# A third buffer for the q and k rows in a fused attention and expert layer: row transfers spread over the slots, expert weights issued by ScalarE

## The chip, the cores and the metric

The kernel runs on one core of one Trainium2 chip. The metric is the device time of one execution in microseconds (us). A profile records one execution; its span runs from the first to the last instruction. PE is TensorE, PEld its weight load, DVE VectorE, ACT ScalarE, POOL GpSimd, SP SyncE; SPq and ACTq are the sequencers of SP and ACT, where DMA issues stand.

## What is computed

The input is 1024 tokens of width 256, layer-normed, and the output adds two branches to it. Cut to what matters:

```python
q, k, v = heads(xn @ Wq.T), heads(xn @ Wk.T), heads(xn @ Wv.T)      # 16 heads of 16
scores = einsum('bhid,bhjd->bhij', q, k) / sqrt(16)                  # 1024 x 1024, causal
std_out = out_proj(softmax(masked(scores)))
qg, qd = splat_feats(q); kg, kd = splat_feats(k)                     # 8 "splats" a head: exp and tanh
splat_attn = (amps*qg) @ kg.T + strength * (amps*qg*qd) @ (kg*kd).T
gsa_out = out_proj(softmax(masked(scores + sensitivity * splat_attn)))
attn = (1 - blend) * std_out + blend * gsa_out
# experts: 16, top 2 of sqrt(softplus(xn @ gate_w.T)), at most 128 tokens each
h = silu(buf @ W1.T) * (buf @ W3.T);  out = h @ W2.T                 # 256 -> 176 -> 256
shared = (silu(xn @ Ws1.T) * (xn @ Ws3.T)) @ Ws2.T
return x + attn + gathered(out) + shared
```

## The kernel before

**Prologue.** The tokens are normed, transposed and projected to q and k (`proj`), the splat features of q and of k are made from these (`feat`), then v and the gate's logits. Attention needs q, k and features as bf16, so each float32 half (q, k, q features, k features, two halves each: eight in all, the order is `SPLIT_ORDER`) is split into three bf16 parts whose sum is the float: ACT writes part 0 (`part0`), a subtraction makes the rest (`rest_of`), ACT writes part 1 (`part1`), and another subtraction makes part 2 (`third_of`, signalled by `part_done`). DVE does six of the first subtractions and two thirds; POOL does six thirds (`POOL_THIRDS` and `LATE`) and the first subtraction of the two late halves (`late_rest_of`). `product(s)` multiplies two features on DVE.

**Rows.** A matmul of a head contracts over 96 rows in SBUF: the three parts of 16 dimensions, repeated so that the wanted products of parts meet, and two rows more for a shift. DMAs copy the parts from `split` into the tiles of the list `stage`: `qs` and `ks` (q and k rows), `fq` and `fk` (feature rows). `RUNS` says which parts go to which rows. One group of two heads takes 12 DMAs of q and k (`load_rows`, `load_qk`), 18 of features (`load_features`) and one for two rows of `fq` (`load_gaps`). Each tile holds two groups: `pr = g % 2` is the group in use, `1 - pr` the next. SP issues all q and k rows and the features of a group's first head; POOL issues the features of the second head.

**Maxima and shift.** Softmax is made safe by the row maxima of the scores, which are found one group ahead. The tasks `max2` and `max` are matmuls on PE into a PSUM bank and a DVE reduction of it; they need the next group's q and k rows (`qk_in`). `shift` turns the maxima (`mhl`, `mT`), and `shift_rows` writes them as two rows under `qs`.

**Main loop.** There are 8 groups. A group has 6 pairs of key blocks, a pair has 4 slots, so 24 slots. In each pair PE runs `pv` of the pair before (weights times v), `splat(0)`, `splat(1)` (adds the feature product to the scores in PSUM), then `std(0)` and `std(1)` of the next pair (q times k). ACT takes the exponential of the scores after `std` and again after `splat`. `splat` waits for the first exponential, the next `std` for the second, `pv` for both. Other work is put into slots by hand in `PLAN`: at slot n of a group every engine does its part of the tasks listed there. The lists are these: maxima of the next group in slots 5 to 7 and 9 to 19, shifts in 9 and 21; routing in group 0; the shared expert in groups 0 and 1 (`sgu`, `shT`, `sy`); four experts in each of the groups 2 to 5 with `xT`, `gu`, `hT`, `y` at slots f+1, f+2, f+4, f+5 for f = 0, 5, 10, 15; the additions of expert outputs in the groups 6 and 7. A `gu` is a matmul on PE, a tanh on ACT, two multiplications on DVE. Three PSUM banks serve these tasks in turn (`place`).

**SP's order.** SP reads the same plan. In group g it first waits until all splats of group g-1 are done (`gsa_ready`) and issues its share of the features of g+1. At `shift` it waits for the shift and issues two small DMAs; at `y` it waits for the expert's output, stores it, and issues the weights of expert a+3 (`expert_in`, two DMAs into the buffer that expert a has just left). At slot 21 (`RELOAD`) it waits until all `std` of the group are done and issues the 12 rows of q and k of group g+2, into the buffer that group g has just left:

```python
if at == RELOAD and g + 2 < NG:
    sp.wait_ge(std_ready, (g + 1) * NU)
    load_qk(g + 2, g % 2)
```

Since group g+1 starts right after slot 23 of group g, and its slot 5 needs these rows, they have some five slots.

**A branch.** If a bound on the features is large (`wide`), a slow way to find the maxima is taken. With these inputs it is not; PE, DVE and SP each load the flag and jump over that code. On PE and DVE the jump stands right ahead of the main loop; the code jumped over is written out eight times, once a group.

## Time and profile before

| | us |
|---|---|
| median of 3 runs | 453.52 (452.94 to 457.52) |
| the profiled execution | 457.28 |
| its span | 455.5 |
| PE busy in it | 353.4 (78%) |
| DVE busy | 233.8 (51%) |
| ACT busy | 194.5 (43%) |
| POOL busy | 114.8 (25%) |
| granted TensorE clock, mean | 0.875 |

All times below are of the profiled execution, counted from the start of its span. A clock of 1.00 is 2.4 GHz, 0.50 is 1.2 GHz. The prologue takes until 83 us; the main loop starts with the first `std` at 83.31. Groups then begin at about 136, 182, 231, 279, 328, 378 and 416 us.

### The profile page before, as it was taken

The page shows a single profiled execution, that of the slowest core. Times are in us where ns is not written, and L with a number is a line of the kernel's source. Part 1 is how long each engine was busy: PE and PEld are TensorE (multiplying, and loading weights), DVE is VectorE, ACT ScalarE, POOL GpSimd, SP SyncE. Part 2 cuts the span into 40 slices and gives each one's busy share as a digit, 9 for nine tenths or more (in the row PEclk, how much of TensorE's full clock was granted, in tenths as well). Part 3 has the DMA queues.
Part 4 walks back from the last instruction along what each step waited for, and adds up shares of the span by engine and source line. Part 5 has one row for each costly group of instructions (what it writes and reads, how often), then busy time and mean ns, then how long its engine had stood idle before and what let it go on. Part 6 is the DMA issues. An engine that isn't in the chain of part 4 may idle for free.

```text
span 455.5 us, 6183 instructions
## 1 busy us (share of the span) xinstructions
PE 353.4 (78%) x2172; PEld 178.8 (39%) x2172; DVE 233.8 (51%) x609; ACT 194.5 (43%) x277; POOL 114.8 (25%) x158
## 2 busy tenths in 40 slices
PE   1996962598975989599976988499928995698984
PEld 1532730244433534254434444344515442333442
DVE  5436579157742664256533664275515751477413
ACT  1874733343433344425350455044522535266830
POOL 5211563400057341400050005010310008720000
PEclk9997955578989799969995999799986999599996
DMA  6233230640035351752275425543385006620011
GB/s 194 95 44 60 26 61 1 81 58 8 0 97 76 43 47 51 110 101 81 72 143 71 141 72 108 89 110 106 88 95 104 21 13 110 171 56 3 0 47 46
DMA packets 28131, 33.02 MB, mean 72 GB/s; under 512 B 8033, under 2 KB 21537, under 8 KB 28097
## 3 DMA queue, kind: packets, MB, share of 16 engines
q1 hardware_dynamic: 21601, 25.16, 25.5%
q0 software_dynamic: 5072, 7.38, 11.5%
q8 instruction: 19, 0.31, 0.3%
q10 hardware_dynamic: 1424, 0.04, 0.2%
q14 instruction: 15, 0.12, 0.1%
HBM read 15.60 MB, written 4.28 MB: 44 GB/s over the span
## 4 chain that ended last, share of the span: by engine, by line
PE 55%; SPq 15%; DVE 14%; ACT 6%; DMA 5%; issue 4%; DVEq 0%; ACTq 0%
SPq L293 13%; PE ps L821 11%; PE ps L749 6%; DVE mx L1096 5%; PE ps L792 5%; PE ps L722 5%; PE ps L758 5%; ACT arena_p L640 5%; PE ps L804 4%; DMA stage<-split 3%; PE ps L680 3%; PE ps L777 2%; PE ps L699 2%; DVE w_sb L917 1%; PE ps L762 1%
## 5 line engine op out<-in xcount | busy, mean ns | idle before, releaser
L640 ACT ACTIVATE arena_p<-ps 128x1024 f32<-128x1024 f32 (+1 forms) x192 | 147.4, 811 | 125.7 <-PE ps L804 97.4
L1096 DVE TENSOR_REDUCE mx<-ps 128x1 f32<-128x512 f32 (+3 forms) x160 | 89.4, 592 | 35.0 <-PE ps L724 29.2
L821 PE MATMUL ps<-arena_p,v_full 128*32 128x512 f32 (+3 forms) x768 | 74.7, 508 | 0.6 <-ACT arena_p L640 0.6
L722 PE MATMUL ps<-stage 96*128 96x512 bf16 (+3 forms) x160 | 57.8, 399 | 13.4 <-DVE mx L1096 11.2
L792 PE MATMUL ps<-stage 98*128 98x512 bf16 (+1 forms) x192 | 54.9, 354 | 15.5 <-ACT arena_p L640 10.9
L804 PE MATMUL ps<-stage 98*128 98x512 bf16 (+1 forms) x192 | 48.8, 340 | 4.5 <-ACT arena_p L640 4.1
L301 POOL DMA_DIRECT2D stage<-split x48 | 27.0, 620 | 76.9 <-PE ps L804 65.3
L387 POOL DMA_INDIRECT wt<-xn_scratch,ids_sb x16 | 15.7, 984 | 116.7 <-PE ps L739 111.5
L645 ACT ACTIVATE small<-ps 128x176 f32<-128x176 f32 x24 | 7.6, 318 | 79.1 <-PE ps L749 79.1
L714 PE MATMUL ps<-stage 96*128 96x128 bf16 (+1 forms) x32 | 8.4, 337 | 42.0 <-DMA stage<-split 42.0
L722 PEld LDWEIGHTS ps<-stage 96*128 96x128 bf16 x160 | 16.9, 109 | 46.0 <-issue 23.3
L821 PEld LDWEIGHTS ps<-arena_p,v_full 128*32 128x32 f32 x768 | 20.4, 111 | 36.2 <-issue 31.2
L758 PE MATMUL ps<-arena_o,small 88*128 88x256 f32 x96 | 30.3, 444 | 4.3 <-DVE small L1119 4.2
L792 PEld LDWEIGHTS ps<-stage 98*128 98x128 bf16 x192 | 19.6, 104 | 35.1 <-ACT arena_p L640 15.7
L1091 DVE TENSOR_REDUCE mx<-ps 128x1 f32<-128x128 f32 x16 | 4.6, 288 | 44.3 <-PE ps L716 44.3
L795 PE MATMUL ps<-mask_t,ident_b 128*128 128x128 bf16 x128 | 26.5, 226 | 0.0
L395 POOL DMA_INDIRECT ids_scratch<-tok,sidx x16 | 15.5, 967 | 43.2 <-DVE sidx L1050 38.6
L804 PEld LDWEIGHTS ps<-stage 98*128 98x128 bf16 x192 | 16.1, 102 | 24.9 <-issue 12.4
L724 PE MATMUL ps<-mask_n,ident_b 128*128 128x128 bf16 x96 | 24.1, 251 | 0.0
L758 PEld LDWEIGHTS ps<-arena_o,small 88*128 88x128 f32 x96 | 18.5, 213 | 13.0 <-DVE small L1119 8.7
L749 PE MATMUL ps<-w_sb,wt 128*128 128x352 f32 x64 | 22.9, 481 | 0.0
L348 POOL TENSOR_TENSOR split<-rest,split 128x1024 bf16<-128x1024 f32 x6 | 12.9, 2152 | 36.2 <-ACT split L582 29.3
(190 smaller groups left out, 466.2 us busy)
## 6 DMA issues: line engine op xcount, KB each, us to landing
w_sb<-in_w_dram SPq DMA_DIRECT2D x16, 352.0 KB
stage<-split SPq DMA_DIRECT2D x40, 96.0 KB
arena_o<-in_w_dram SPq DMA_DIRECT2D x16, 176.0 KB
stage<-split SPq DMA_DIRECT2D x40, 64.0 KB
ye_scratch<-wt SPq DMA_DIRECT2D x16, 128.0 KB, 1.8
stage<-split SPq DMA_DIRECT2D x56, 32.0 KB
acc<-in_x_dram SPq DMA_DIRECT2D x2, 512.0 KB, 4.5
wt<-in_wqkvo_dram SPq DMA_DIRECT2D x4, 256.0 KB, 6.4
```

Source lines behind the costliest of these rows:

```text
L293: eng.dma_start(stage[n][row:row + num * HD, pr, h, :], src).then_inc(done, 16)
L301: eng.dma_start(stage[n][row + w:row + num * HD:2, pr, h, :], split[p0:p0 + NS, 2, part:part + 1, w, :].to_broadcast((NS, num, T))).then_i ...
L640: A(to, ps[:, 1 + 2 * s:3 + 2 * s, off:CH], ACT.Exp, scale=SCALE).then_inc(done, 1)
L722: ins = M(b[:, 0:n1 - n0], lhs, ks[0:KR, pr, h, n0:n1], start=True, stop=not diag)
L724: ins = M(b[:, n1 - n0 - P:n1 - n0], ident_b[:, :], mask_n[:, :], start=False, stop=True)
L749: ins = M(b[:, 0:2 * I], lhs, w13_sb[:, wb, k, :], start=k == 0, stop=k == KD - 1)
L758: ins = M(b[:, 0:D], hT[:, c, :], w2_sb[:, wb, c, :], start=c == 0, stop=c == 1)
L792: ins = M(b[:, off:CH], ks[:, pr, h, (jb + s) * P:(jb + s + 1) * P], qs[:, pr, h, ic * CH + off:(ic + 1) * CH], start=True, stop=not diag)
L795: ins = M(b[:, off:off + P], ident_b[:, :], mask_t[:, :], start=False, stop=True)
L804: ins = M(ps[:, 1 + 2 * s + h, off:CH], fk[:, pr, h, (jb + s) * P:(jb + s + 1) * P], fq[:, pr, h, ic * CH + off:(ic + 1) * CH], start=Fals ...
L821: ins = M(ps[c:c + 2 * HD, 0, off:CH], v_full[:, jb + s, g * GH + h, :], of, start=jb + s == 0, stop=end)
L1096: V.reduce_max(mx[:, it // TC, h, it % TC, pc:pc + 1], b[:, 0:n1 - n0], AX.X).then_inc(aux_free, 1)
```

## The change

- `qs` and `ks` hold three groups (`QB = 3`), `g % QB` is the group in use. The 12 row transfers of group g+2 go out in slots 0 to 11 of group g, one a slot. The feature rows of both heads and the gap row (19 in all) go out in slots 2 to 20 of group g, one a slot, all from SP. The only wait ahead of them is `gsa_ready` at slot 0. POOL issues no rows.
- The weights of experts 3 to 15 are issued by ACT, in the slot of a `gu`, right behind its tanh. The weights of experts 0 to 2 stay with SP.
- The maxima lie in slots 0 to 5 and 6 to 20, the shifts in 8 and 22.
- Prologue: another `SPLIT_ORDER`, no `LATE` halves; DVE does all eight first subtractions and thirds 0 to 3, POOL thirds 4 to 7, and the rests of halves 4 to 7 lie in `arena_p`. PE makes both feature sets without a break, then takes the branch, then the first maxima (`max0`) and v. DVE takes the branch ahead of `max0`. In the branch PE and DVE run a hardware loop over the groups in place of the eight copies. SP issues the q and k rows of group 1 ahead of the features of group 0.

```diff
-        stage = [sb(f"stage{n}", [KS, 2, GH, T], bf16) for n in range(4)]
+        stage = [sb(f"stage{n}", [KS, QB if n < 2 else 2, GH, T], bf16) for n in range(4)]
...
-        SPLIT_ORDER = [(0, 0), (1, 0), (2, 0), (2, 1), (3, 0), (3, 1), (0, 1), (1, 1)]
-        LATE = (6, 7)
-        POOL_THIRDS = (1, 2, 3, 5)
+        SPLIT_ORDER = [(0, 0), (1, 0), (0, 1), (1, 1), (2, 0), (2, 1), (3, 0), (3, 1)]
+        POOL_THIRDS = (4, 5, 6, 7)
...
-        maxima = spread(max0, 5, 7) + [(9, ("shift", 0))] + spread(max1, 9, 19) + [(21, ("shift", 1))]
-        RELOAD = 21
+        maxima = spread(max0, 0, 5) + [(8, ("shift", 0))] + spread(max1, 6, 20) + [(22, ("shift", 1))]
...
             for g in range(NG):
-                if g < NG - 1:
-                    if g:
-                        sp.wait_ge(gsa_ready, g * NU)
-                    load_features(sp, g + 1, 1 - g % 2, 2, F_SP, f_in[1 - g % 2])
-                    load_features(sp, g + 1, 1 - g % 2, 3, F_SP, f_in[1 - g % 2])
-                    load_gaps(g + 1, 1 - g % 2)
...
                             sp.dma_start(ye_d[a * CAP:(a + 1) * CAP, :], ye[:, a % YB, :]).then_inc(ye_out[a % YB], 16)
-                            if a + WB < E:
-                                expert_in(a + WB)
...
-                    if at == RELOAD and g + 2 < NG:
-                        sp.wait_ge(std_ready, (g + 1) * NU)
...
-                        load_qk(g + 2, g % 2)
+                    if g and at == 0:
+                        sp.wait_ge(gsa_ready, g * NU)
+                    if g + 2 < NG and at < N_QK:
+                        load_qk_row(sp, g + 2, (g + 2) % QB, at, qk_in[(g + 2) % QB])
+                    if g + 1 < NG and 2 <= at < 2 + N_F:
+                        load_feature_row(sp, g + 1, (g + 1) % 2, at - 2, f_in[(g + 1) % 2])
...
                                 A(th, ps[:, bank, 0:I], ACT.Tanh, scale=0.5).then_inc(th_ready, 1)
+
+                            if kind == "gu" and 1 <= a and a - 1 + WB < E:
+                                e = a - 1 + WB
+                                act.wait_ge(aux_free, count_of("y", a - 1))
+                                act.dma_start(w13_sb[:, e % WB, :, :], w13[e, :, :].rearrange("(k p) i -> p k i", p=P)).then_inc(w_in[e % WB], 16)
+                                act.dma_start(w2_sb[:, e % WB, :, :], w2[e, :, :].rearrange("(k p) d -> p k d", p=I2)).then_inc(w_in[e % WB], 16)
...
-                for g in range(NG):
-                    pe.wait_ge(own_in, (g + 1) * (16 * 30))
+                with pe.Fori(0, NG) as g:
+                    pe.wait_ge(own_in, (g + 1) * (16 * (N_QK + N_F - 1)))
...
+            pe.wait_ge(qk_in[0], 16 * N_QK)
+            for t in max0:
+                aux(-1, t, 0)
+            prologue(n_v)
+            aux(-1, ("shift", 0), 0)
```

Three places show what moved. The first is SP's queue at the end of a group with experts (`stage0` and `stage1` are `qs` and `ks`, `stage2` and `stage3` are `fq` and `fk`, L457 is the shift, L513 an expert's output). Before:

```order
L513 DMA ye_scratch<-wt 128x256 [waits aux_free]
L497 DMA w13_sb<-in_w13_dram 128x2x352
L498 DMA arena_o<-in_w2_dram 88x2x256
L457 DMA stage0<-mT 2x4x128 [waits aux_free]
L457 DMA stage0<-mT 2x4x128
L293 DMA stage0<-split 48x1x1024 [waits part_done7,part_done6,std_ready]
L293 DMA stage0<-split 32x1x1024
L293 DMA stage0<-split 16x1024
```

After, at the same place:

```order
L308 DMA stage3<-split 16x1x1024
L483 DMA ye_scratch<-wt 128x256 [waits aux_free]
L311 DMA stage2<-gap_scratch 2x2048
L427 DMA stage0<-mT 2x4x128 [waits aux_free]
L427 DMA stage0<-mT 2x4x128
L295 DMA stage0<-split 48x1x1024 [waits gsa_ready]
L295 DMA stage0<-split 32x1x1024
L295 DMA stage0<-split 16x1024
L302 DMA stage2<-split 24x1x1024
```

The weights are gone from the queue, the 12 rows no longer wait for the last `std` of their own buffer, and the gap row of the next group stands behind the wait for the group's last expert. The rows that follow are those of the group after the next.

The second is ACT in a group with experts (arena_p takes the exponentials, `small` the tanh). Before:

```order
L640 ACTIVATE arena_p<-ps 128x2x384 [waits std_ready]
L640 ACTIVATE arena_p<-ps 128x1024 [waits gsa_ready]
L645 ACTIVATE small<-ps 128x176 [waits aux_full]
L640 ACTIVATE arena_p<-ps 128x2x384 [waits gsa_ready]
L640 ACTIVATE arena_p<-ps 128x2x256 [waits std_ready]
```

After:

```order
L608 ACTIVATE arena_p<-ps 128x2x384 [waits std_ready]
L608 ACTIVATE arena_p<-ps 128x1024 [waits gsa_ready]
L613 ACTIVATE small<-ps 128x176 [waits aux_full]
L618 DMA w_sb<-in_w_dram 128x2x352 [waits aux_free]
L619 DMA arena_o<-in_w_dram 88x2x256
L608 ACTIVATE arena_p<-ps 128x2x384 [waits gsa_ready]
L608 ACTIVATE arena_p<-ps 128x2x256 [waits std_ready]
```

Two DMA issues stand between the tanh and the next exponential.

The third is DVE in the prologue (L924 and L896 are first subtractions, L1153 and L1126 the product, L1091 and L1096 reductions of the maxima). Before:

```order
L1153 SCALAR_TENSOR_TENSOR arena_o<-arena_o,par 128x1024 [waits pro_act]
L924 SCALAR_TENSOR_TENSOR rest<-arena_o,par,split 128x1024 [waits part_done0,first_part]
L924 SCALAR_TENSOR_TENSOR rest<-arena_o,split 128x1024 [waits part_done1,first_part]
L1091 TENSOR_REDUCE mx<-ps 128x1 [waits aux_full]
L1092 TENSOR_REDUCE mx<-ps 128x1
```

After:

```order
L889 TENSOR_TENSOR split<-rest,split 128x1024 [waits second_part,second_rest] x2
L1126 SCALAR_TENSOR_TENSOR arena_o<-arena_o,par 128x1024 [waits pro_act]
L896 SCALAR_TENSOR_TENSOR arena_p<-arena_o,par,split 128x1024 [waits first_part]
L896 SCALAR_TENSOR_TENSOR arena_p<-arena_o,split 128x1024 [waits first_part]
L889 TENSOR_TENSOR arena_o<-arena_o 128x1024 [waits pro_act]
L896 SCALAR_TENSOR_TENSOR arena_p<-arena_o,split 128x1024 [waits first_part] x2
L1142 TENSOR_LOAD wide [waits wide_ready]
L1142 ISA x2
L1143 COMPARE_AND_BRANCH
```

All subtractions and the branch now come ahead of the first reduction; before, the reductions of `max0` stood after four of them and the branch after all maxima.

## Rows read from the trace of the kernel before

**Rows 1.** The chain that ended last, by engine and by line, from the page.

```profile
PE 55%; SPq 15%; DVE 14%; ACT 6%; DMA 5%; issue 4%; DVEq 0%; ACTq 0%
SPq L293 13%; PE ps L821 11%; PE ps L749 6%; DVE mx L1096 5%; PE ps L792 5%; PE ps L722 5%; PE ps L758 5%; ACT arena_p L640 5%; PE ps L804 4%; DMA stage<-split 3%; PE ps L680 3%; PE ps L777 2%; PE ps L699 2%; DVE w_sb L917 1%; PE ps L762 1%
```

**Rows 2.** Waits: engine, line, releaser; us in total, times, longest us.

```profile
PE ps L714 <- DMA stage<-split: 42.0, 7, 8.7
ACT arena_p L640 <- PE ps L804: 97.4, 37, 11.3
```

**Rows 3.** Timeline of PE: start, us, engine, line; idle before and its releaser.

```profile
37.58 0.23 PE L714 MATMUL ps<-stage 96*128 96x128 bf16 x1 [3.22 <-DMA stage<-split]
...
148.06 0.29 PE L714 MATMUL ps<-stage 96*128 96x128 bf16 x1 [4.34 <-DMA stage<-split]
...
342.94 0.29 PE L714 MATMUL ps<-stage 96*128 96x128 bf16 x1 [8.67 <-DMA stage<-split]
```

**Rows 4.** Windows: us, busy us (instructions) of PE, PEld, DVE, ACT, POOL; PEclk, DMA share, GB/s.

```profile
148.00:158.00 10.00, 9.82 (x54) 5.58 (x55) 6.55 (x18) 3.66 (x5) 3.06 (x3) 0.70 0.34 35
...
194.50:204.00 9.50, 9.41 (x48) 5.69 (x48) 5.55 (x16) 1.64 (x4) 0.99 (x1) 0.61 0.52 89
...
243.20:251.40 8.20, 8.19 (x36) 5.09 (x40) 4.87 (x13) 0.80 (x3) 0.99 (x1) 0.61 0.45 61
251.40:281.50 30.10, 28.04 (x198) 14.16 (x199) 18.14 (x46) 15.94 (x21) 6.44 (x11) 1.00 0.38 106
...
391.60:400.00 8.40, 8.36 (x54) 4.44 (x55) 6.37 (x18) 4.45 (x5) 6.27 (x8) 0.72 0.61 146
```

**Rows 5.** Timeline of SP's queue, at the start of group 0 and from group 3 to 4.

```profile
81.02 12.93 SPq L293 DMA_DIRECT2D stage<-split  x12
...
276.56 0.34 SPq L513 DMA_DIRECT2D ye_scratch<-wt  x1
276.94 0.44 SPq L497 DMA_DIRECT2D w_sb<-in_w_dram  x1
277.42 0.44 SPq L498 DMA_DIRECT2D arena_o<-in_w_dram  x1
...
279.23 10.65 SPq L293 DMA_DIRECT2D stage<-split  x12
```

**Rows 6.** Timeline around one tanh and one expert's end: ACT and PE.

```profile
261.40 0.32 ACT L645 ACTIVATE small<-ps 128x176 f32<-128x176 f32 x1 [4.02 <-PE ps L749]
261.61 3.77 ACT L640 ACTIVATE arena_p<-ps 128x1024 f32<-128x1024 f32 x4
...
262.69 0.61 PE L804 MATMUL ps<-stage 98*128 98x512 bf16 x2 [0.40 <-ACT arena_p L640]
...
278.99 0.59 PE L804 MATMUL ps<-stage 98*128 98x512 bf16 x2
```

**Rows 7.** Timeline of the prologue: POOL and DVE.

```profile
60.91 4.21 POOL L355 TENSOR_TENSOR rest<-xx,split 128x1024 f32<-128x1024 f32 x2
...
61.93 3.35 DVE L1004 SCALAR_TENSOR_TENSOR w_sb<-w_sb 128x128 f32<-128x128 f32 x1
...
70.36 4.07 DVE L917 TENSOR_TENSOR w_sb<-w_sb 128x128 f32<-128x128 f32 x2
```

**Rows 8.** Timeline of the prologue: ACT, PE and DVE, and the branch.

```profile
37.64 1.06 ACT L582 ACTIVATE split<-rest 128x1024 bf16<-128x1024 f32 x1
...
48.37 7.17 PE L699 MATMUL ps<-wt,xx 128*128 128x256 f32 x32
55.38 4.03 PE L673 MATMUL ps<-gw_sb,xx 128*128 128x16 f32 x32
...
65.34 3.13 DVE L1096 TENSOR_REDUCE mx<-ps 128x1 f32<-128x512 f32 x6
...
83.29 0.29 DVE L917 TENSOR_TENSOR g_last<-w_sb,gb_sb 128x128 f32<-128x128 f32 x1 [3.74 <-issue]
...
83.31 0.58 PE L792 MATMUL ps<-stage 98*128 98x512 bf16 x1 [4.33 <-issue]
```

252 lines of the change are left out of this document (111 added, 141 removed).

## The prediction

> **What bounds the kernel now.** I read the chain that ended last first. PE carries 55% of the span, which is no surprise with PE busy for 78% of it; but SP's queue carries 15%, 13% of it at L293, the issue of q and k rows, and the row transfers another 3% [rows 1]. An engine that computes nothing holds some 18% of the time. The waits say where: PE at L714, the first maxima task of the next group, waits for a transfer into the row tiles seven times, 42.0 us in total [rows 2]. In PE's timeline one of the seven is in the prologue, 3.22 us; the other six are one in each of the groups 1 to 6, from 4.34 to 8.67 us [rows 3]. They add up to 42.0 - 3.2 = 38.8 us. Group 0 has none, and group 7 has no maxima.
>
> The cause stands in SP's queue. From group 3 to 4, the last expert's output goes at 276.56, its weights at 276.94 and 277.42, two shift rows follow, and only at 279.23 do the 12 rows start, which take 10.65 us [rows 5]. Group 4 has itself begun by then: its first `splat` runs at 278.99 [rows 6]. The rows are needed some five slots later and can't come earlier, since they go into the buffer that group 3 has just left.
>
> The windows show a second cost behind the wait. In the 8 to 10 us after each of the six waits the granted clock is between 0.61 and 0.72 (four of the six are shown), while in the rest of a group it is 1.00 [rows 4]. PE is busy without a gap there, 8.19 of 8.20 us from 243.2, so the time is PE's own work at a lower clock. At full clock a window of length w and clock c would take w x c: the loss is 3.0 us (10 x 0.30), 3.7, 3.2 and, in the last, 2.4 us; the two not shown give 2.8 each. That is 17.9 us. Of TensorE's two levels, 1.2 GHz is what is granted for most of these windows, after an idle stretch of 4 to 9 us.
>
> So a group of some 48 us holds about 6.5 us of wait and 3 us of slow clock. The undisturbed stretch from 251.4 to 281.5 has PE busy for 28.04 of 30.10 us at clock 1.00 [rows 4]: once the wait is gone, PE itself is the bound there.
>
> **The change part by part.**
>
> *Third buffer and spread rows.* The rows of group g+2 go out in the first half of group g, into a buffer that group g-1 has left, and are needed in slot 0 of group g+1. Twelve rows take 10.65 us on SP, and 12.93 at their slowest [rows 5], against a group of nearly 40 us. All six waits end: -38.8 us. With them goes the slow stretch: -17.9 us.
>
> *What SP now has to carry.* A group has 12 q and k rows, 18 feature rows (9 before) and the gap row. I have no row for 31 in a run, so bounds: at 10.65/12 = 0.89 us each they take 27.5 us, at 12.93/12 = 1.08 us each 33.4 us; four shift rows and four expert outputs add about 4. That is 32 to 37 us in a group that I expect to last about 42, so SP keeps up, but with little room. One place is tight. The gap row stands behind the wait for the last expert (slot 20), and the next group's first `splat` needs it. Before, the expert's output was issued at 276.56 and that `splat` ran at 278.99, 2.4 us later. The gap row would be issued next, at about 276.94, and take roughly 0.4 us to issue; of its landing I only know that output stores and rows land in about 2 us. It comes at about 279.4: 0.4 us late, in four or five groups. I put +2 us on this (0 to 5).
>
> *Expert weights on ACT.* Thirteen experts, each with two issues. On SP they took 0.44 us each [rows 5], so 0.9 us a pair and 11.7 us for all, now between a tanh and the next exponential. Is ACT's idle time the cover? ACT waits for PE's L804 for 97.4 us [rows 2], but not there: before its tanh it sits 4.02 us idle for the matmul of `gu`, while exponentials queue behind the tanh. After the one at 261.40 come four exponentials without a gap, 3.77 us, and PE's `splat` at 262.69 already waits 0.40 us for them [rows 6]. So a pair ahead of them is mostly on the path. Only in slot 7 does a long `pv` (slots 2, 12 and 17 have none between) give cover. I take 0.85 of 11.7: +10 us. Ends: 0 (all hidden) and 13 x 2 = +26 us, if an issue on ACT takes 1 us, the slowest row of SP's. The short wait it adds for the last expert's output costs nothing: DVE has done that before PE could start this `gu`, as `gu` waits for the later `xT`.
>
> A rule of the Trainium skill speaks here. *DMA: Bandwidth & Descriptors*, section on issuing engines, says that issues from several engines run on the same 16 DMA engines, and that using more of them only saves the issuing sequencer's time. The trace agrees as far as it goes (the same transfers in the window from 251.4 with a DMA share of 0.38), so the move to ACT earns nothing by itself.
>
> *Features off POOL.* POOL's issues were not on the chain [rows 1], 0.
>
> *Maxima over 21 slots instead of 14.* The tasks are the same. In the stretch after the wait DVE was busy for 4.87 of 8.20 us [rows 4], which would be nearly all of it once PE runs at full clock (8.2 x 0.61 = 5.0 us). Spreading them takes that away. I count 0, within 3 us.
>
> *Prologue.* This I worked out as a chain, and the result is nearly nothing. Before, DVE had its first late maxima at 59.9 and the last at 77.8, then the branch cost PE 4.33 us up to the first `std` at 83.31 and DVE 3.74 us [rows 8]. In that stretch DVE twice ran into POOL: a 128x128 operation of 0.3 us took 3.35 us beside POOL's 4.21, and two took 4.07 us [rows 7]. Some 6.5 us of that go, because POOL's work is done earlier. After, the steps are: (1) from 27 us ACT has 11 conversions of 1.06 us [rows 8], 8 feature evacuations of about 0.65 and two projections of 1.0, and waits for a product for about 2.5: 48 us; the last subtraction ends at 49. (2) The branch on DVE, 3.7 us: 52.7. (3) The first maxima and shift: 3.9 us, 56.7. (4) The v and gate matmuls, 7.17 + 4.03 = 11.2 us [rows 8], which ran beside ACT's and DVE's work before and now stand between the first and the later maxima. A quarter of v is ahead of the shift, but PE has sat idle for most of the time from 40 to 53, so I add about 3 us for a slow clock: 70. (5) Sixteen maxima at 3.13/6 = 0.52, with gaps 0.58 us, 9.3 us, and the gate's DVE work, 4.5 us: 83.9. The first `std` comes at about 84, against 83.31: +1 us. If the shorter code makes the jump cheap it is 81 (-2.5), if PE's clock stays low for all of v and gate 89 (+6).
>
> The lock between DVE and POOL is also in the Trainium skill (*SBUF — State Buffer*, on the shared port pair: an exclusive lock for a whole instruction). By a plain sharing of bandwidth the 0.3 us operations would take 0.6; the row shows 3.35, so the whole of the excess goes with the overlap.
>
> *Sum,* against the profiled execution: 457.3 - 38.8 - 17.9 + 2 + 10 + 1 = 413.6 us. That execution is 3.8 us above the median of 453.52. In proportion, 413.6 x 453.5 / 457.3 = 410.2; less the same 43.7 us, 409.8. I say 411.
>
> **The rivals.**
>
> *The ACT issues are hidden.* For it: 97.4 us of ACT waiting for PE [rows 2]. Against it: the queue of exponentials behind each tanh. Time: 411 - 10 = 401 us.
>
> *The wait moves to the feature rows.* SP has 31 rows a group and everything behind one queue, and the share of the DMA engines reached 0.52 even behind the waits [rows 4]. For it: the slowest rate shown, 1.08 us a row, brings SP to 37 us of 42. Against it: half the rows then have a group to spare. If PE waits 3 us for features at each of six starts, and gets the slow clock back for 2 us each time: +30, 441 us.
>
> *The clock gives back little.* The stretch after a wait could be paced by DVE's reductions or ACT's queue rather than by PE. For it: DVE 4.87 us in what would be 5.0. Against it: PE has no gap there. If only a quarter of 17.9 comes back: 411 + 13 = 424 us. A page of the Trainium skill points this way: *TensorE: Matmul & The Clock Gate*, section on HAM oscillation, has an example in which each wait for a transfer is followed by 1.67 us at half speed, half of which is lost; six of those would be 5 us, an estimate from the page, and the time by it 424. The windows here measure more, 17.9 us, and I go by them.
>
> *Nothing moves.* The transfers, not their issue, were late, and stay late under the same load: 453 us. Against it: the share of the DMA engines is only 0.38 in the stretch from 251.4 [rows 4], and the rows will go out there.
>
> *Slower.* Place: ACT, behind the tanh. If an issue on ACT is held while the DMA engines work off the rows that SP now sends all through the group, the exponentials behind it are late, and PE gets the lower clock as well, as it did behind the wait of 4.34 us. Price: a pair must cost 13 x p > 56.7 - 3, so p above 4.1 us. At p = 5 us, 454 - 57 + 3 + 65 = 465 us. Nothing shows such an issue: SP's own slowest, at a full load, is 1.08 us.
>
> **How the numbers follow.** Forecast 0.60; ACT hidden 0.12; wait at the features 0.14; clock gives back little 0.08; nothing 0.03; slower 0.03. The predicted time is the forecast's, 411. The range takes in the hidden ACT (401), the clock rival (424), the upper ends of the ACT price and of the prologue taken one at a time, and leaves out the 441: 400 to 429. A measurement of this kernel tells about 1% from no change. Faster by over 1%: 0.60 + 0.12 + 0.14 + 0.08 = 0.94; within 1%: 0.03; slower: 0.03.
>
> **What would show it.** Right: no wait of PE at the first maxima task for a transfer; a window of clock 1.00 through all of the groups 2 to 5; groups 2 to 5 of 42 to 43 us; ACT issues of 0.4 to 0.5 us on its queue and a PE wait for ACT of under 1 us behind each `gu`; a first `std` between 81 and 89. The ACT price is wrong if groups 2 to 5 are not 3 to 4 us longer than group 6, which has no experts. The whole is wrong if `splat(0)` of a group waits for a transfer for over 2 us, or if the clock stays under 0.8 without any wait.

## The result and the profile after

The changed kernel takes 411.88 us (median of 4 runs, 407.55 to 413.09) against 455.52 us before (median of 4). The ratio is 0.902, 95% interval 0.893 to 0.912. The profiled execution took 413.09 us, 44.2 us less than that of before (457.28). In the experiments one execution of `rows_burst` (566.19 us at a granted clock of 0.561) and two of `act_early_again` (397 us at 0.93) are left out of the ratios as slow. The forecast was 411, in a range from 400 to 429. The sum came out right; its terms did not, and two of them missed by 6 and 8 us in opposite directions.

The page of the profile after, engines and the chain that ended last (before: [rows 1]):

```profile
PE 339.2 (82%) x2172; PEld 173.6 (42%) x2172; DVE 234.2 (57%) x613; ACT 194.3 (47%) x277; POOL 66.2 (16%) x82
...
PE 67%; DVE 15%; ACT 10%; issue 3%; ACTq 3%; DMA 1%; DVEq 0%; SPq 0%
```

SP's queue went from 15% of the chain to nothing, PE from 55% to 67%. New is ACT's queue with 3%: some 12 us in which the end waited for a DMA issue on ACT.

The waits of PE after (us in total, times, longest; before: [rows 2]):

```profile
PE ps L766 <- ACT arena_p L608: 13.5, 15, 2.1
PE ps L778 <- ACT arena_p L608: 11.6, 12, 1.7
```

There is no row with a transfer any more; the 42.0 us at the first maxima are gone. At the top stand the matmuls of `std` (L766) and of `splat` (L778), waiting for exponentials.

The windows show where the time went. A stage ends where DVE copies the second shift (`mT`) of a group: the prologue, then groups 0 to 6; group 7 is the rest of the span. The bounds of these windows lie up to 0.7 us behind the copies. Columns as in [rows 4]. After:

```profile
0.00:78.30 78.30, 53.15 (x207) 29.00 (x208) 46.88 (x113) 40.39 (x59) 18.80 (x33) 0.84 0.41 80
78.30:127.70 49.40, 41.58 (x241) 20.06 (x242) 31.44 (x105) 20.78 (x30) 6.72 (x7) 0.84 0.30 55
127.70:168.60 40.90, 37.10 (x253) 18.90 (x251) 22.88 (x59) 19.12 (x28) 11.92 (x13) 0.96 0.35 60
168.60:214.80 46.20, 40.21 (x263) 20.23 (x262) 24.18 (x64) 19.55 (x28) 3.78 (x4) 0.93 0.41 90
214.80:257.80 43.00, 36.46 (x260) 18.87 (x258) 24.15 (x63) 19.55 (x28) 3.78 (x4) 1.00 0.46 113
257.80:302.10 44.30, 37.24 (x268) 19.76 (x266) 25.45 (x65) 19.66 (x28) 3.78 (x4) 1.00 0.47 109
302.10:343.20 41.10, 36.47 (x259) 18.87 (x258) 24.16 (x63) 19.34 (x28) 1.89 (x2) 1.00 0.40 85
343.20:370.70 27.50, 25.39 (x214) 11.56 (x212) 20.47 (x51) 18.06 (x25) 15.50 (x16) 1.00 0.45 112
```

From copy to copy groups 2 to 5 take 45.7, 43.0, 44.3 and 41.1 us, 174.1 in all. The same stages before took 79.3, 54.8, 46.2, 47.9, 48.2, 48.8, 50.6 and 38.6 us at clocks between 0.79 and 0.93. Group 7 did not change (41.1 and 40.9 us). So groups 1 to 6 gave back 280.3 - 243.0 = 37.3 us, and the prologue with group 0 gave 134.13 - 127.46 = 6.7 us. At full clock PE is busy for about 36.5 us in a group with experts, but groups 2 to 5 take 41 to 46 us. Group 1, with only the shared expert, takes 41.0. What lies between is the subject of the experiments.

### The profile page after: what moved, and what is told of

Read it like the earlier page. It is cut to its first block, busy times and chain, and to the rows that moved or that the text cites. A ratio compares the mean times of both kernels' runs of the same rounds, so it can differ in the third digit from the quotient of the medians.

```text
span 411.3 us, 6179 instructions
## 1 busy us (share of the span) xinstructions
PE 339.2 (82%) x2172; PEld 173.6 (42%) x2172; DVE 234.2 (57%) x613; ACT 194.3 (47%) x277; POOL 66.2 (16%) x82
## 4 chain that ended last, share of the span: by engine, by line
PE 67%; DVE 15%; ACT 10%; issue 3%; ACTq 3%; DMA 1%; DVEq 0%; SPq 0%
PE ps L795 16%; PE ps L723 8%; PE ps L766 7%; ACT arena_p L608 7%; DVE mx L1069 6%; PE ps L732 5%; PE ps L778 5%; PE ps L696 5%; PE ps L654 4%; ACTq L619 2%; PE ps L751 2%; PE ps L673 2%; PE ps L769 2%; ACT small L613 2%; PE ps L736 1%
## 5 line engine op out<-in xcount | busy, mean ns | idle before, releaser
L608 ACT ACTIVATE arena_p<-ps 128x1024 f32<-128x1024 f32 (+1 forms) x192 | 145.8, 811 | 96.6 <-PE ps L778 58.5
L1069 DVE TENSOR_REDUCE mx<-ps 128x1 f32<-128x512 f32 (+3 forms) x160 | 92.1, 592 | 78.2 <-PE ps L698 53.9
L766 PE MATMUL ps<-stage 98*128 98x512 bf16 (+1 forms) x192 | 51.9, 337 | 14.2 <-ACT arena_p L608 13.5
L778 PE MATMUL ps<-stage 98*128 98x512 bf16 (+1 forms) x192 | 46.8, 334 | 11.6 <-ACT arena_p L608 11.6
L370 POOL DMA_INDIRECT wt<-xn_scratch,ids_sb x16 | 15.2, 950 | 157.7 <-PE ps L713 154.5
L696 PEld LDWEIGHTS ps<-stage 96*128 96x128 bf16 x160 | 15.6, 99 | 45.7 <-issue 26.2
L766 PEld LDWEIGHTS ps<-stage 98*128 98x128 bf16 x192 | 18.6, 100 | 34.1 <-ACT arena_p L608 22.4
L732 PE MATMUL ps<-arena_o,small 88*128 88x256 f32 x96 | 27.8, 415 | 5.4 <-DVE small L1092 5.3
L778 PEld LDWEIGHTS ps<-stage 98*128 98x128 bf16 x192 | 16.5, 99 | 28.5 <-ACT arena_p L608 16.2
L698 PE MATMUL ps<-mask_n,ident_b 128*128 128x128 bf16 x96 | 22.2, 231 | 0.0
L400 POOL DMA_INDIRECT xx<-ye_scratch,gidx x16 | 15.5, 969 | 33.8 <-issue 33.8
L1120 DVE COPY pv_sb<-ps 128x512 f32<-128x512 f32 x16 | 11.0, 690 | 16.6 <-PE ps L795 16.1
L1088 DVE SCALAR_TENSOR_TENSOR small<-small,ps 128x176 f32<-128x176 f32 x24 | 8.1, 338 | 20.4 <-ACT small L613 20.4
L889 DVE TENSOR_TENSOR acc<-ps,acc 128x256 f32<-128x256 f32 (+1 forms) x14 | 7.5, 538 | 18.1 <-PE ps L751 13.3
```

The costliest lines, as they stand in the source:

```text
L608: A(to, ps[:, 1 + 2 * s:3 + 2 * s, off:CH], ACT.Exp, scale=SCALE).then_inc(done, 1)
L696: ins = M(b[:, 0:n1 - n0], lhs, ks[0:KR, pr, h, n0:n1], start=True, stop=not diag)
L698: ins = M(b[:, n1 - n0 - P:n1 - n0], ident_b[:, :], mask_n[:, :], start=False, stop=True)
L732: ins = M(b[:, 0:D], hT[:, c, :], w2_sb[:, wb, c, :], start=c == 0, stop=c == 1)
L766: ins = M(b[:, off:CH], ks[:, pr, h, (jb + s) * P:(jb + s + 1) * P], qs[:, pr, h, ic * CH + off:(ic + 1) * CH], start=True, stop=not diag)
L778: ins = M(ps[:, 1 + 2 * s + h, off:CH], fk[:, pr, h, (jb + s) * P:(jb + s + 1) * P], fq[:, pr, h, ic * CH + off:(ic + 1) * CH], start=Fals ...
```

## The experiments

Times are medians, each with its ratio to the kernel before on the same chip. A theory or rival is named as in the text on record above it. The stages of one kernel are compared with those of another by their marks (the `mT` copies), and I write them from group 1 on.

### The changed kernel again, and another chip

The first four variants ran on a chip on which the kernel before took 476.34 us, the slower chip below. The next four, the changed kernel among them, ran on a chip on which the kernel before took 457.39 us, and the last four on a third with 456.20 us.

> The changed kernel itself, unaltered, so that the other kernels of this call have it on the same chip. In the first call of experiments the kernel before took 476 us and not 454, and all four variants showed waits for "issue" of 11 to 13 us near the start of group 7 and of 1.4 to 3.4 us in group 1, which the changed kernel's first profile does not have. Theory A (those waits belong to that chip, whatever the variant): if the kernel before takes about 454 us here, this takes 408 to 413 us and has no such waits; if it takes about 476 us, this takes 428 to 434 us and has them. Rival B (they came with the variants): 408 to 413 us on any chip.

Measured: 411.90 us, before 457.39 (ratio 0.899, 0.894 to 0.903). No such wait: theory A as far as this chip goes. On the slower chip the changed kernel itself was not run, so I compare the variants from there only by groups 2 to 5. That this is fair is shown by one kernel that ran on both chips (below): 39.3, 39.4, 39.6, 39.4 us on the slower chip, 39.3, 39.4, 39.7, 39.4 on the third. And `unrolled_branch`, whose main loop is that of the changed kernel, takes 172.3 us for groups 2 to 5 on the slower chip, against 174.1 and 174.2 us in the two profiles of the changed kernel; 1.7 us of the difference is the clock.

### The third buffer alone

```diff
+    QB = 3
...
-        RELOAD = 21
+        RELOAD = 5
...
-                        sp.wait_ge(std_ready, (g + 1) * NU)
-                        load_qk(g + 2, g % 2)
+                        load_qk(g + 2, (g + 2) % QB)
```

> The kernel before with the third buffer alone: the q and k rows of group g + 2 are issued in one burst at slot 5 of group g into the third buffer, with no wait for the standard deviations; the prologue, the slots of the maxima, the features on GpSimd and the weights on SyncE stay as before. Theory A (the prediction's waits -38.8 and slow clock -17.9 are the third buffer's, and the weights on ScalarE and the prologue are costs): 50 to 57 us less than the kernel before, about 0.88 of it, and less than after_again. Rival B (without the weights moved from SyncE the burst of 24 rows holds the gap row or the weights, as the weights on SyncE held the gap row in weights_on_sp): PE waits for the gap row of 2 us or more in several groups, and 30 to 42 us less than the kernel before.

Measured: 404.14 us (ratio 0.883, 0.881 to 0.885), 53.3 us less than before and 7.8 less than the changed kernel. Theory A. The whole of the gain, and more, comes with this one part. PE's waits, and group 3:

```profile
PE ps L792 <- ACT arena_p L640: 10.9, 20, 0.8
...
PE ps L714 <- DMA stage<-split: 3.2, 1, 3.2
```

```profile
214.00:253.40 39.40, 36.49 (x260) 18.80 (x258) 24.06 (x65) 19.18 (x29) 9.04 (x13) 1.00 0.58 123
```

Of the seven waits at L714 only the one in the prologue is left. Groups 1 to 6 take 39.8, 39.4, 39.5, 40.1, 39.4 and 28.2 us at clock 1.00, 226.4 in all, 53.9 less than before. PE had waited 38.8 us there, so the other 15.1 us came with the clock. The gap row is no trouble here, and rival B falls: as in the kernel before, SP issues that of the next group at the start of a group, a whole group ahead of its use.

### Everything but the early rows

```diff
-        maxima = spread(max0, 0, 5) + [(8, ("shift", 0))] + spread(max1, 6, 20) + [(22, ("shift", 1))]
+        maxima = spread(max0, 5, 7) + [(9, ("shift", 0))] + spread(max1, 9, 19) + [(21, ("shift", 1))]
-                    if g + 2 < NG and at < N_QK:
-                        load_qk_row(sp, g + 2, (g + 2) % QB, at, qk_in[(g + 2) % QB])
+                    if g + 2 < NG and at == 21:
+                        sp.wait_ge(std_ready, (g + 1) * NU)
+                        for j in range(N_QK):
+                            load_qk_row(sp, g + 2, (g + 2) % QB, j, qk_in[(g + 2) % QB])
```

> The changed kernel with the use of the third buffer taken back in time only: the maxima stand in their old slots, and the q and k rows of group g + 2 are issued by SyncE in one burst at slot 21, behind the standard deviations of group g + 1, as before the change. Theory A (the gain is the time at which the rows are issued, and not that the features are in one piece or that the weights moved): PE again waits 5 to 7 us for rows at the first maxima of each group, with 3 us of slow clock behind each; 40 to 55 us more than after_again. Rival B (the features' move or the unbroken prologue is what saves): within 10 us of after_again.

Measured: 444.82 us (444.53 without the execution of 566 us; ratio 0.971, 0.969 to 0.974), 32.6 more than the changed kernel. Rival B falls, but theory A's 40 to 55 us was too much. PE's timeline, three of its six waits for rows:

```profile
141.22 0.29 PE L690 MATMUL ps<-stage 96*128 96x128 bf16 x1 [3.61 <-DMA stage<-split]
...
236.51 0.23 PE L690 MATMUL ps<-stage 96*128 96x128 bf16 x1 [2.03 <-DMA stage<-split]
...
379.58 0.29 PE L690 MATMUL ps<-stage 96*128 96x128 bf16 x1 [5.09 <-DMA stage<-split]
```

The six sum to 18.0 us, not 38.8. Groups 1 to 6 take 30.5 us more than in the changed kernel beside it; the rest beyond the waits goes with the clock, 0.87 to 0.95 in five of the six groups, and with PE's waits for exponentials (28.2 us against 24.6). The burst starts sooner behind the group's end (no weights ahead of it) and its 12 rows take 7.6 us of SP's time and not 10.65 [rows 5]. The waits are halved by a lighter queue and ended only where the third buffer lets the rows go out early.

### The weights: on SP, or ahead of the tanh on ACT

In the first variant the two lines of `expert_in` go back behind the store at `y`. In the second they stay on ACT and move from behind the tanh to ahead of it:

```diff
                         for kind, a in PLAN[g][4 * p + turn]:
+                            if kind == "gu" and 1 <= a and a - 1 + WB < E:
+                                e = a - 1 + WB
+                                act.wait_ge(aux_free, count_of("y", a - 1))
+                                act.dma_start(w13_sb[:, e % WB, :, :], w13[e, :, :].rearrange("(k p) i -> p k i", p=P)).then_inc(w_in[e % WB], 16)
+                                act.dma_start(w2_sb[:, e % WB, :, :], w2[e, :, :].rearrange("(k p) d -> p k d", p=I2)).then_inc(w_in[e % WB], 16)
                             if kind in ("gu", "sgu"):
                                 bank, count = place(g, (kind, a))
                                 act.wait_ge(aux_full, count)
                                 A(th, ps[:, bank, 0:I], ACT.Tanh, scale=0.5).then_inc(th_ready, 1)
-                            if kind == "gu" and 1 <= a and a - 1 + WB < E:
-                                e = a - 1 + WB
...
```

> The changed kernel, but with the weights of experts 3 to 15 issued by SyncE again, behind the store of the expert output, as before the change. Theory A (the 13 pairs of issues sit on the path through ScalarE): the prediction put +10 us on them, and the changed kernel's trace shows about 1.2 us for a pair, so some 15 us of issue time of which most delays the exp behind it and through it TensorE; without them groups 2 to 5 become 2 to 4 us shorter each and the time is about 397 to 402 us, the PE waits behind each gate (0.8 to 2.2 us now) fall under 0.8 us. Rival B (the issues are hidden, ScalarE has slack): 411 to 413 us, the same as the changed kernel. Rival C (SyncE has no room for 26 more issues beside the rows of two groups): the wait for rows comes back at the maxima, 415 us or more.

> The changed kernel with one thing moved: on ScalarE the two weight issues stand ahead of the tanh's wait for the gate's matmul instead of behind the tanh. In the changed kernel's trace ScalarE idles there before each tanh, and is needed at once behind it. Theory A (what costs is where the issues stand): most of their price goes, 398 to 404 us. Rival B (what costs is that they are on ScalarE at all, since it must catch up anyway, or that issues are slow beside SyncE's): 409 to 413 us. If the wait for the previous expert's last matmul ends later than the gate's own, the tanh itself is held and the time rises above 413 us.

Measured, on the slower chip: 437.82 us on SP (ratio 0.920, 0.915 to 0.925), 426.74 us ahead of the tanh (0.895, 0.891 to 0.900). By groups 2 to 5, which take 174.1 us in the changed kernel: 167.7 us on SP, 157.7 ahead of the tanh. On SP the waits of 0.8 to 2.2 us behind the gates fell to 0.8 at most, as theory A had it, but only 6.4 us came of it, since PE waited 6.5 us for the gap row in their place, and the clock fell behind two of these waits (below). The wait for rows at the maxima of rival C did not come. Of the second kernel theory A holds. It ran again on the third chip:

> The kernel of weights_act_early again: the changed kernel with ScalarE's weight issues ahead of the tanh's wait. In the first call its groups 2 to 5 took 39.2 to 39.8 us each at full clock, where the changed kernel's take 41 to 46 us, but that call's chip added about 20 us in groups 1 and 6. Theory A (the place of the issues behind the tanh costs the changed kernel some 16 us): if the kernel before takes about 457 us here, this takes 394 to 399 us, 0.865 of it. Rival B (part of the gain was that chip's): 402 to 412 us.

Measured: 390.96 us (ratio 0.857, 0.854 to 0.860), before 456.20. Theory A, even below its range. It takes 390.5 to 391.0 us at a mean clock of 0.952 and 397 us at 0.93; the changed kernel takes 412 us at 0.929 and 408 us at 0.94. So at a like clock the gain over the changed kernel is some 15 to 17 us rather than 21. It is faster than both kernels of this case.

What the placement does is seen in ACT's timeline. The changed kernel, an expert of group 3; `small` is the tanh, L618 and L619 the issues, L608 the exponentials; and PE, which waits behind them:

```profile
249.34 0.32 ACT L613 ACTIVATE small<-ps 128x176 f32<-128x176 f32 x1 [3.63 <-PE ps L723]
249.34 0.38 ACTq L618 DMA_DIRECT2D w_sb<-in_w_dram  x1
249.76 1.11 ACTq L619 DMA_DIRECT2D arena_o<-in_w_dram  x1
250.92 2.22 ACT L608 ACTIVATE arena_p<-ps 128x1024 f32<-128x1024 f32 x3 [1.26 <-DVE small L1089]
```

```profile
252.00 0.28 PE L766 MATMUL ps<-stage 98*128 98x256 bf16 x1 [2.15 <-ACT arena_p L608]
```

The tanh ends at 249.66; the exponential behind it started at 250.92, as soon as the issues were through, and PE stood 2.15 us for it. (The releaser that the row names, DVE's `small`, is the multiplication behind this same tanh. It raises the semaphore on which ACT waits for the last expert's output, but the count that ACT needs had been reached before.) The same place with the issues ahead of the tanh:

```profile
230.08 0.81 ACT L608 ACTIVATE arena_p<-ps 128x768 f32<-128x768 f32 x1 [0.51 <-PE ps L769]
230.09 0.43 ACTq L613 DMA_DIRECT2D w_sb<-in_w_dram  x1
230.56 0.44 ACTq L614 DMA_DIRECT2D arena_o<-in_w_dram  x1
234.53 0.32 ACT L618 ACTIVATE small<-ps 128x176 f32<-128x176 f32 x1 [3.63 <-PE ps L723]
234.74 2.68 ACT L608 ACTIVATE arena_p<-ps 128x1024 f32<-128x1024 f32 x4
```

ACT idles 3.63 us ahead of its tanh in both. The issues now lie in that idle time, and the exponentials follow the tanh without a gap. Its PE waits, and its groups 2 and 3:

```profile
PE ps L766 <- ACT arena_p L608: 7.1, 15, 0.8
...
PE ps L778 <- ACT arena_p L608: 5.2, 8, 1.3
```

```profile
162.30:201.60 39.30, 36.38 (x259) 18.82 (x259) 24.07 (x63) 19.07 (x28) 3.78 (x4) 1.00 0.46 106
201.60:241.00 39.40, 36.48 (x259) 18.92 (x260) 24.11 (x64) 19.20 (x29) 3.78 (x4) 1.00 0.48 124
```

Groups 2 to 5 take 157.7 us against 174.1 in the changed kernel: 16.4 us is what 13 pairs behind the tanh cost. PE's waits for `arena_p` fell from 25.1 to 12.3 us over the whole kernel and from 20.3 to 7.3 in groups 2 to 5, which is 13.0 of it; the other 3.4 us is the clock, 0.50 for 6.8 us in group 2.

### Issues with no load behind them

Weights on SP, and behind each of 13 tanhs:

```diff
+                                for w in range(2):
+                                    act.dma_start(tiny_d[(2 * a + w) * P:(2 * a + w + 1) * P, :], ident[:, 0:1]).then_inc(tiny_out, 16)
```

> The weights are issued by SyncE as in weights_on_sp, and ScalarE issues two DMAs of 512 bytes each (one column of the identity, to a scratch tensor that nothing reads) behind each of the 13 tanhs instead. They take ScalarE's time for an issue and next to none of the DMA engines'. Theory A (issue time on ScalarE alone is the price): the time is near the changed kernel's, 408 to 413 us. Rival B (it is the queue of large transfers or their order that costs): near weights_on_sp, within 2 us. The second issue of a pair took 0.44 to 1.50 us in the changed kernel; if it stays above 0.7 us with tiny transfers, the length is set by something other than the size of the transfer.

Measured, on the slower chip: 455.67 us (ratio 0.957, 0.950 to 0.964), 17.9 us more than weights_on_sp on the same chip. Its 26 issues:

```profile
L621 ACTq DMA_DIRECT2D tiny_scratch<-ident x26: 326/393/1222, 192.8 to 338.5; - x26
```

They sum to 12.0 us. Theory A: the price is the time that ACT spends on issuing, 26 x 0.46 us here, plus what it pulls behind it, and not the transfers. The rival with the large transfers falls. Groups 2 to 5 take 17.5 us more than in `weights_on_sp`: PE's waits for exponentials there rose from 7.3 to 17.0 us, those for the gap row from 6.5 to 11.2 us, and the lower clock took 3.4 us more. Why the gap row is later still is open.

### Why the weights had to leave SP: the gap row

`weights_on_sp` has nothing behind ACT's tanh and was still slower than the kernel with the issues ahead of it; PE waited for the gap row. The next run asks whether the later shift is to blame: weights on SP, maxima and shifts in their old slots.

> The changed kernel with the weights on SyncE as in weights_on_sp and the maxima and shifts in their old slots. In weights_on_sp PE waited 2.0 to 2.3 us for the gap row in groups 2 to 4; in before_third_buffer, with weights on SyncE too, it never did. Theory A (the later shift, slot 22 and not 21, together with the weights on SyncE makes the gap row late): no wait for gap_scratch here, groups 2 to 5 of 39 to 40 us, and 397 to 400 us, before_third_buffer's 404.1 less the shorter prologue. Rival B (the rows of one per slot beside the weights are what holds the gap row): the waits of 2 us stay, 404 to 410 us.

Measured: 407.06 us (ratio 0.893, 0.890 to 0.896). Rival B: the waits stay. SP's queue at the end of group 2, and PE's wait for it:

```profile
206.74 0.35 SPq L483 DMA_DIRECT2D ye_scratch<-wt  x1
207.13 0.43 SPq L473 DMA_DIRECT2D w_sb<-in_w_dram  x1
207.94 0.31 SPq L474 DMA_DIRECT2D arena_o<-in_w_dram  x1
208.30 0.27 SPq L311 DMA_DIRECT2D stage<-gap_scratch  x1
```

```profile
211.47 1.03 PE L775 MATMUL ps<-stage 98*128 98x512 bf16 x2 [2.28 <-DMA stage<-gap_scratch]
```

With the weights on ACT (act_early_again) the same place reads:

```profile
201.56 0.32 SPq L483 DMA_DIRECT2D ye_scratch<-wt  x1
201.93 0.29 SPq L311 DMA_DIRECT2D stage<-gap_scratch  x1
```

The gap row is issued 0.4 us behind the expert's store instead of 1.6 us, with 528 KB of weights not ahead of it, and PE has no wait for it. The later place in the queue is 1.2 us of the 2.28; that the weights also slow the row's transfer is likely, but no run separates it. With weights on SP three groups lose 2.2 to 2.3 us each, and the clock falls to 0.96 there: 43.3, 44.0 and 42.9 us a group.

### The spread of the maxima

> act_early_again with one thing undone: the maxima and shifts stand in their old slots (5 to 7, 9 to 19, shifts at 9 and 21) instead of spread over slots 0 to 22. Theory A (the prediction's: the spread is worth nothing, 0 with 3 us to either side): within 3 us of act_early_again. Rival B (the spread evens VectorE's load and is needed for groups of 39 us): 5 us or more slower, with waits for DVE mx in groups 2 to 5. Rival C (the old slots release the gap rows earlier and let VectorE finish): 1 to 4 us faster.

Against `act_early_again` the edit is the line of `maxima` shown above. Measured: 398.22 us (ratio 0.872, 0.868 to 0.875). By the medians rival B, by the groups theory A: groups 1 to 6 take 39.8, 39.4, 39.4, 40.1, 39.4 and 28.2 us, in the spread version 39.3, 39.3, 39.4, 39.7, 39.4 and 28.0, 1.4 us in all. Of the rest 4.5 us is group 0, 51.0 us against 46.4, 1.3 us the prologue and 0.6 us group 7. But group 0 of the spread kernels took between 46.4 and 50.0 us in seven profiles, so that I can't say how much of those 4.5 us the spread earned; the three kernels with the old slots and the new prologue took 50.9 to 51.0. `sp_old_maxima` and this kernel differ only in the place of the weights: 8.8 us for taking them off SP.

This kernel also tells what is left of the price of ACT's issues. Its groups 1 to 6 take 226.4 us, as those of `before_third_buffer` do, and groups 2 to 5 take 158.3 us in both. There the weights are on SP and half the features on POOL; here all features are on SP and the weights on ACT, ahead of the tanh. Neither move costs anything that can be seen in these groups.

### The weights on ACT in the kernel before

```diff
-                            if a + WB < E:
-                                expert_in(a + WB)
...
                                 A(th, ps[:, bank, 0:I], ACT.Tanh, scale=0.5).then_inc(th_ready, 1)
+                            if kind == "gu" and 1 <= a and a - 1 + WB < E:
+                                e = a - 1 + WB
+                                act.wait_ge(aux_free, count_of("y", a - 1))
+                                act.dma_start(w13_sb[:, e % WB, :, :], w13[e, :, :].rearrange("(k p) i -> p k i", p=P)).then_inc(w_in[e % WB], 16)
+                                act.dma_start(w2_sb[:, e % WB, :, :], w2[e, :, :].rearrange("(k p) d -> p k d", p=I2)).then_inc(w_in[e % WB], 16)
```

> The kernel before with the weights on ScalarE alone, placed behind the tanh as in the change. Theory A (the issues' price on ScalarE is paid wherever PE runs without a wait for rows, as the prediction's +10 has it): 5 to 12 us slower than the kernel before. Rival B (PE waits for the rows of its next group anyway, SyncE's burst has 26 issues fewer beside it, and rows_burst was 12.6 us faster than the kernel before with a prologue 5 us shorter): 3 to 8 us faster. Rival C: the two cancel, within 2 us.

Measured: 465.57 us (ratio 1.022, 1.018 to 1.027), 9.4 us slower. Theory A in size, but not by itself: PE's six waits for rows fell from 38.8 to 28.2 us, as rival B had it, and the issues took more than that back: PE's waits for exponentials rose from 15.0 to 28.7 us. The move by itself is a loss.

### The branch

First the kernel before with hardware loops:

```diff
-                for g in range(NG):
+                with pe.Fori(0, NG) as g:
...
-                for g in range(NG):
+                with dve.Fori(0, NG) as g:
```

> The kernel before with the bodies of TensorE's and VectorE's branch on the random-feature matrix written as a hardware loop over the groups instead of eight times; nothing else. Theory A (the length of the code jumped over sets the branch's price): TensorE's 4.33 us and VectorE's 3.7 us behind the branch shrink to under 1.5 us, the first standard deviation ends 2.5 to 4.3 us earlier than at 83.3 us, and the time falls by as much. Rival B: no change, within 1 us of the kernel before.

Measured: 454.69 us (ratio 0.995, 0.992 to 0.998), 2.7 us faster. PE and DVE behind the branch, where before they stood 4.33 and 3.74 us [rows 8]:

```profile
80.87 0.29 DVE L917 TENSOR_TENSOR g_last<-w_sb,gb_sb 128x128 f32<-128x128 f32 x1 [0.71 <-ACT w_sb L627]
```

```profile
80.95 0.59 PE L792 MATMUL ps<-stage 98*128 98x512 bf16 x1 [1.35 <-issue]
```

Theory A: the first `std` starts 2.4 us earlier. Then the changed kernel with the bodies written out.

> The changed kernel with the bodies of TensorE's and VectorE's branch on the random-feature matrix written out eight times instead of a hardware loop over the groups, as before the change; the features stay in one piece. Theory A (the length of the code that a branch jumps over sets its price: 4.33 us on TensorE before, at most 1.4 us after, and VectorE's fell too): the first standard deviation ends 2 to 5 us later than the 78.3 us of the changed kernel, and the time is 2 to 5 us more, 414 to 417 us. Rival B (the branch costs nothing to speak of, the features in one piece made the prologue shorter): within 1 us of the changed kernel.

Measured, on the slower chip: 441.49 us (ratio 0.926, 0.921 to 0.931). The total says nothing without the changed kernel on that chip, but PE's timeline does. The second fence is the changed kernel:

```profile
49.37 0.29 PE L688 MATMUL ps<-stage 96*128 96x128 bf16 x1 [9.54 <-issue]
```

```profile
45.30 0.29 PE L688 MATMUL ps<-stage 96*128 96x128 bf16 x1 [4.82 <-issue]
...
50.86 0.61 PE L696 MATMUL ps<-stage 96*128 96x512 bf16 x1 [3.89 <-DVE mx L1065]
```

Written out, PE stands 4.7 us longer (with loops the wait is 4.8 us on the slower chip as well), so the length of the body sets the price here too. But with loops PE soon waits 3.89 us for DVE, which is free only at 50.2; the prologue ends at 77.8 us here and at 76.6, 77.3 and 78.1 in the three kernels with loops that ran beside it. Theory A holds for the jump and fails for the time: the new place of the branch hides it.

## Why the prediction was right, step by step

| term | predicted | measured | by |
| --- | --- | --- | --- |
| waits for rows and slow clock behind them | -56.7 | -53.9 | groups 1 to 6 of before_third_buffer |
| gap row late | +2 | 0 | no wait; 6.5 to 6.8 if the weights stay on SP |
| weights on ACT | +10 | +16.4 | groups 2 to 5, against act_early_again |
| features off POOL, maxima spread | 0 | +0.2 | what is left in groups 1 to 6: -1.4 for the spread, +1.6 in group 1 at a clock of 0.96 |
| prologue (and group 0) | +1 | -6.7 | marks at 134.13 and 127.46 |
| sum | -43.7 | -44.2 | profiled executions (-0.2 in group 7) |

The forecast of 411 against 411.88 is luck in part: the weights came out 6.4 us dearer than forecast and the prologue with group 0 7.7 us cheaper.

*Third buffer.* Right. The six waits and most of the slow clock came back, in the kernel before by itself and at the full price. The rival in which the clock gives back little falls: 15.1 us beside the 38.8 against the forecast 17.9. One reading of rows was wrong, and nothing hung on it: the share of the DMA engines behind the waits reached 0.61 in [rows 4], not 0.52. The Trainium skill's example (*TensorE: Matmul & The Clock Gate*, HAM oscillation) would have made it 5 us, an estimate from its figure; the measurement decides, and it goes with the windows of [rows 4].

*The gap row* did not come late, though it was predicted tight by 0.4 us. It was issued at once behind the expert's store, as the step said, and PE never waited for it. That the step was worth making is shown by the variants with weights on SP. The prediction weighed the cost of leaving SP but missed this use: it said that the move "earns nothing by itself", on the Trainium skill's rule on issuing engines (*DMA: Bandwidth & Descriptors*). In the kernel before that holds (9.4 us slower); beside one-a-slot rows it earns 8.8 us when placed well.

*Weights on ACT.* The mechanism was right and the size was off: +10 predicted, +16.4 measured, inside the bound of +26. The first mis-sized term is the duration of a pair, taken as 0.9 us from SP's queue. These two rows are the changed kernel's issues (ns, least, median, most):

```profile
L618 ACTq DMA_DIRECT2D w_sb<-in_w_dram x13: 379/382/402, 182.7 to 316.7; - x13
...
L619 ACTq DMA_DIRECT2D arena_o<-in_w_dram x13: 437/752/1498, 183.2 to 317.1; - x13
```

They sum to 5.0 and 10.4 us, 1.18 us a pair: the second issue of a pair is the dear one. The share that PE felt was forecast rightly: 13.0 us of waits are 0.85 of these 15.4. With the issues ahead of the tanh the sum is 11.4 us. The second part that was missed is the clock: behind a PE wait of 1.71 us for such an exponential it fell for 6.8 us in group 2,

```profile
196.00:198.00 2.00, 2.00 (x11) 1.05 (x11) 0.64 (x2) 1.67 (x2) 0.00 (x0) 0.73 0.76 254
198.00:200.00 2.00, 2.00 (x6) 1.37 (x6) 0.69 (x1) 1.02 (x1) 0.00 (x0) 0.50 0.01 3
```

while waits of 1.4 to 2.15 us in groups 3 to 5 left it at 1.00. In `after_again` the same wait of 1.71 us left it at 1.00, and one of 2.20 us in group 3 was followed by 3.4 us at 0.50. Of the signs that the prediction named, a PE wait of under 1 us behind each `gu` came out wrong (0.8 to 2.15 us), and so did groups 2 to 5 of 42 to 43 us and of clock 1.00: they are 45.7, 43.0, 44.3 and 41.1 us, the first at 0.93. The sign against group 6 can't tell anything: that group takes 28.0 us here and 27.9 with the issues ahead of the tanh, since PE has only 25.4 us of work in it. The rival "ACT issues are hidden" was false for this place and true some 4 us earlier in ACT's own queue.

*Prologue.* Wrong by 6 to 8 us, the largest error, and it cancelled the one above. The first `std` came at 78.29 us, not 84, and below the sign of 81 to 89. Step 2 failed: DVE's last first subtraction ended at 50.28, later than the 49 of step 1, but the first reduction of `max0` ran at 50.20, so DVE's branch cost nothing instead of 3.7 us. Step 3 gave that back: the first shift was copied at 56.34 us, where 56.7 was forecast. What came early was step 4. PE did a quarter of v ahead of the shift at the slow clock and the rest at full clock:

```profile
52.37 3.73 PE L673 MATMUL ps<-wt,xx 128*128 128x256 f32 x8
...
56.23 5.80 PE L673 MATMUL ps<-wt,xx 128*128 128x256 f32 x24
```

The gate followed and ended at 65.5 us, where 70 was forecast, so the 3 us that the step added for a slow clock behind the shift did not come. Step 5 took 12.8 us instead of 13.9. Against the kernel before, what left the path at the end of the prologue is the jump, which cost PE 4.33 us there; the prediction had named the short body as a possible gain (81, -2.5) and taken the other value. DVE and POOL still collide once. DVE, with a subtraction of the same size that runs alone first, then POOL:

```profile
40.65 1.23 DVE L896 SCALAR_TENSOR_TENSOR arena_p<-arena_o,split 128x1024 f32<-128x1024 f32 x1
43.91 2.17 DVE L889 TENSOR_TENSOR arena_o<-arena_o 128x1024 f32<-128x1024 f32 x1 [2.03 <-ACT arena_o L532]
46.00 4.28 DVE L896 SCALAR_TENSOR_TENSOR arena_p<-arena_o,split 128x1024 f32<-128x1024 f32 x2
50.20 0.28 DVE L1064 TENSOR_REDUCE mx<-ps 128x1 f32<-128x128 f32 x1
```

```profile
42.87 5.19 POOL L354 TENSOR_TENSOR split<-arena_p,split 128x1024 bf16<-128x1024 f32 x2 [28.26 <-ACT split L551]
```

The -6.7 us is also one draw of several: in the seven profiles of kernels with the new prologue and the spread maxima, group 0 ended between 123.0 and 128.1 us, 6.0 to 11.2 us ahead of before.

*SP's load and the features.* SP carried 31 rows a group with no PE wait for feature rows in any group; that rival did not come about.

*Left open.* Which part of the 6.7 us is the branch and which the order of the maxima is bounded only: the branch in the kernel before is worth 2.7, the old slots with the new prologue end group 0 at 127.5 to 128.8. Weights issued by GpSimd were not tried.

## What to carry to other kernels

Price a DMA issue by where it stands in its engine's queue, not by the engine's idle share: the same 13 pairs on ACT cost 16 us behind the tanh and nothing measurable ahead of it, where ACT was idle for 3.6 us anyway. When a wait disappears, run that part alone: here one part was worth 53 us and all parts together 45 on the same chip, and a later edit of one placement brought the whole to 391 us. And when a sum comes out right, check its terms in the stages, since two errors of 6 and 8 us cancelled here.

## What the runs showed of the hardware

The clock is not settled by the kernel's own waits. `act_early_again` and `after_again` are the same code up to the end of group 0, and both have a PE wait of 2.18 us that ends at about 118. The windows behind it, first act_early_again, then after_again:

```profile
115.00:120.00 5.00, 2.82 (x25) 1.41 (x24) 3.08 (x14) 1.00 (x3) 2.09 (x3) 1.00 0.44 129
```

```profile
115.00:120.00 5.00, 2.82 (x13) 1.74 (x11) 3.36 (x16) 1.35 (x3) 1.66 (x2) 0.70 0.30 85
```

PE is busy for 2.82 of 5 us in both, at a granted clock of 1.00 in one and 0.70 in the other. Group 0 takes 46.4 us in the first and 48.9 in the second. These two ran on different chips, but it is not the chip alone: `tiny_act_issues` and `weights_on_sp`, also the same code up to there, ran on one chip and took 46.4 and 50.0 us in group 0, at clocks of 0.91 and 0.84. That executions of one kernel fall into two clusters 4 to 6 us apart goes with their mean clock (0.952 and 0.93 for `act_early_again`); only one execution of each is profiled, so in which stretch they part is not shown.

The chips differ in something that is neither the clock nor the groups at work. On the slower one (kernel before: 476 us) all engines but POOL stood still in group 6 for 10 to 12 us while POOL issued its sixteen gathers, in all four kernels profiled there. A stretch of `weights_act_early`:

```profile
351.00:355.00 4.00, 0.00 (x0) 0.00 (x0) 0.00 (x0) 0.00 (x0) 3.09 (x4) 0.50 0.39 111
```

PE's own stop there is 11.09 us, put down to `issue`. Groups 1 and 6 took 52.2 and 48.5 us, against 39.3 and 28.0 for the same kernel on the third chip, and groups 2 to 5 were alike to 0.1 us. While the gathers ran (340.5 to 360.2 us), the trace has one packet of an instruction queue, and the next comes at 377; the changed kernel on its chip has three during its gathers. That fits code loads held behind the gathers, but it is argued, not shown, and the kernel before has no profile on that chip.

Two DMA issues back to back on ACT are unlike: the first took 0.38 to 0.40 us behind the tanh, the second 0.44 to 1.50 us, and with 512-byte transfers issues took up to 1.22 us. What makes the long ones long is not shown.
